# Token tiles turned by VectorE in 32x32 blocks and by transfers inside SBUF, in place of TensorE transposes, in six of eight passes

## What is computed

```python
x = x + 0.5 * ffn0(LN(x))      # silu(x W1^T) * (x W3^T), fast Walsh-Hadamard transform, W2^T; hidden 2048
x = x + attn0(LN(x))           # a second norm with gamma and beta, causal attention, o_proj, its own residual
x = x + 0.5 * ffn0(LN(x))
x = x + 0.5 * ffn1(LN(x))      # ternary weights: silu((x gate^T) gate_s) * ((x up^T) up_s), (down^T) * down_s; hidden 1408
x = x + attn1(LN(x))           # tanh(x B^T) C^T + D * x
x = x + 0.5 * ffn1(LN(x))
```

## Time and profile before

| | us |
|---|---|
| median of 3 runs | 1706.19 |
| lowest, highest | 1705.47, 1707.06 |
| span of the profiled execution | 1703.6 |

### The profile page before, as it was taken

The page is one execution under the profiler, slowest core; times in us unless marked ns, Lnnn a source line. Parts: engine busy times, 40 slices in busy tenths (PEclk is TensorE's granted clock), DMA queues, the critical chain, the costliest instruction groups (busy, mean ns, idle before and its releaser), DMA issues.

```text
span 1703.6 us, 21742 instructions
## 1 busy us (share of the span) xinstructions
PE 1694.7 (99%) x7707; PEld 1401.8 (82%) x7707; DVE 1154.4 (68%) x1808; ACT 830.3 (49%) x1359; POOL 125.5 (7%) x185
## 2 busy tenths in 40 slices
PE   9999999999999999999999999999999999999998
PEld 7788888888888888888888888888888888888887
DVE  8888678677775555754446554447768869877866
ACT  5745444465575543434223333224556556655644
POOL 1000000000012220000000000000000143200001
PEclk9999999999999999999999999999999999999999
DMA  9776665699985000253444433444666763366765
GB/s 317 266 310 247 229 258 211 236 377 369 369 333 207 1 0 1 87 191 126 153 167 167 167 142 136 167 167 146 232 215 211 273 222 112 113 242 234 257 221 213
DMA packets 97341, 344.56 MB, mean 202 GB/s; under 512 B 10192, under 2 KB 25424, under 8 KB 91856
## 3 DMA queue, kind: packets, MB, share of 16 engines
q1 hardware_dynamic: 97232, 343.14, 55.0%
HBM read 261.83 MB, written 81.26 MB: 201 GB/s over the span
## 4 chain that ended last, share of the span: by engine, by line
PE 94%; DVE 3%; DMA 1%; SPq 1%; issue 1%; ACT 0%; DVEq 0%; ACTq 0%
PE psum L561 35%; PE psum L563 30%; PE psum L565 27%; PE psum L857 2%; DMA x<-in_w2a 1%; SPq L705 1%; DVE xc_lo L2074 0%; DMA flat<-in_w3a 0%; DMA w<-w_kept 0%; PE psum L1134 0%; DVE att_lo L2043 0%; DVE fw_lo L2037 0%; SPq L664 0%; DVE x L2020 0%; DVE x L2123 0%
## 5 line engine op out<-in xcount | busy, mean ns | idle before, releaser
L561 PE MATMUL psum<-xc_hi,w 128*128 128x512 f32 x1544 | 604.6, 392 | 0.5 <-DVE psum L2143 0.3
L563 PE MATMUL psum<-xc_lo,w 128*128 128x512 f32 x1544 | 600.9, 389 | 0.0
L565 PE MATMUL psum<-xc_hi,w 128*128 128x512 f32 x928 | 361.3, 389 | 0.0
L561 PEld LDWEIGHTS psum<-xc_hi,w 128*128 128x128 f32 x1544 | 289.8, 188 | 64.4 <-DVE psum L2143 1.6
L563 PEld LDWEIGHTS psum<-xc_lo,w 128*128 128x128 f32 x1544 | 289.9, 188 | 58.8
L561 PE MATMUL psum<-w,hid 128*128 128x512 f32 x864 | 337.5, 391 | 0.0
L565 PE MATMUL psum<-w,hid 128*128 128x512 f32 x864 | 336.4, 389 | 0.0
L2107 DVE TENSOR_TENSOR x<-psum,x 128x512 f32<-128x512 f32 x256 | 173.0, 687 | 148.3 <-PE psum L565 147.7
L563 PE MATMUL psum<-w,hid 128*128 128x512 f32 x544 | 211.7, 389 | 0.0
L565 PEld LDWEIGHTS psum<-xc_hi,w 128*128 128x128 f32 x928 | 174.2, 188 | 36.7
L2131 DVE TENSOR_TENSOR hid<-sg,hid 128x512 fp32r<-128x512 f32 x212 | 144.3, 691 | 85.2 <-ACT hid L1450 83.3
(11 more groups left out here) (177 smaller groups left out, 2030.1 us busy)
## 6 DMA issues: line engine op xcount, KB each, us to landing
w<-w_kept SPq DMA_DIRECT2D x93, 896.0 KB, 6.6
w<-w_kept SPq DMA_DIRECT2D x130, 512.0 KB, 7.1
w<-w_kept SPq DMA_DIRECT2D x57, 640.0 KB, 4.4
w_kept<-w SPq DMA_DIRECT2D x16, 1792.0 KB, 7.3
w<-w_kept SPq DMA_DIRECT2D x93, 256.0 KB, 4.5
w_kept<-prep SPq DMA_DIRECT2D x12, 1792.0 KB, 7.6
w_kept<-w SPq DMA_DIRECT2D x16, 512.0 KB, 6.3
w_kept<-prep SPq DMA_DIRECT2D x12, 512.0 KB, 8.9
```

The source lines that it names most:

```text
L561: pe.matmul(out, a_hi, b_hi, start=start, stop=False, skip_group_check=onto)
L563: last = pe.matmul(out, a_hi, b_lo, start=False, stop=stop and zero == "a", skip_group_check=onto)
L565: last = pe.matmul(out, a_lo, b_hi, start=False, stop=stop, skip_group_check=onto)
```

## The change

Passes 0, 2, 3, 4, 5 and 6 (`SWAPPED`) no longer use TensorE to turn tiles. Pass 1, the attention and the state-space layer keep their transposes.

- VectorE transposes a normalised tile in 32x32 blocks (`swap_pair`, one instruction a tile, two a slot), from xn into the new buffer `swap`, in which the tokens of the pair's two tiles lie alternately (a step of two floats). The pair stands in the slot of its normalisation: in kind B and in A ahead of `sum_c22`, in pass 0 between the two `hid_low`.
- SyncE then moves the blocks to their partitions (`turn_load`): 16 transfers inside SBUF for a pair, each of 32 partitions x 4 runs of 256 B to 32 other partitions, 32 KB. 24 pairs make 384 transfers. In kind B they stand between the first and the later pieces of the weights of slot s+1, at the pair's slot s-1; in kind A and pass 0 behind the slot's loads. They wait for VectorE's swap; the first pair of a kind B pass also for the gates of slot 2, the third and fourth for the down products of slot 4.
- xn has two tiles instead of four; a pair is normalised once the pair before is swapped (in pass 5 also once GpSimd has used it). `norms` of pass 6 become slots 4 to 7.
- The tokens in xs now lie in pairs. Plain order is set where the hidden unit is split: `hid_high` (ScalarE) and `low` (VectorE) read their source with a step of two floats in passes 1, 3, 4, 5, 7 and in the first half of the state-space layer. The planes of xs are renumbered.
- `sums` waits for the transfers. In pass 6 its four steps now stand at the end of slot 8, the start of slot 9, and two at the end of slot 9; in pass 4 they stay.
- ScalarE's 48 copies out of PSUM go.

```diff
-FIRST_SUMS, LAST_SUMS = {8: 0, 9: 2}, {8: 1, 9: 3}
+FIRST_SUMS = {5: {8: (0,), 9: (2,)}, 7: {9: (1,)}}
+LAST_SUMS = {5: {8: (1,), 9: (3,)}, 7: {8: (0,), 9: (2, 3)}}
-NORMS = {4: (3, 4, 5, 6), 5: (4, 5, 6, 7), 6: (4, 4, 5, 6), 7: ()}
+NORMS = {4: (3, 4, 5, 6), 5: (4, 5, 6, 7), 6: (4, 5, 6, 7), 7: ()}
+SWAPPED = (0, 2, 3, 4, 5, 6)
+BLOCK = 32
+LANDED = 16 * 16
-TURNS = {4: (4, 5, 6, 7), 5: (5, 6, 7, 8), 6: (4, 5, 6, 7), 7: ()}
...
+        swap = at("swap", [P, P // BLOCK, KD, BLOCK, 2], F32, "xn", 4 * KIB)
...
+        def in_pairs(tile, no):
+            return tile.rearrange("p (h t i) -> p h i t", h=2, i=2) if paired(no) else tile
...
+                if between:
+                    turn_load(*between)
                 if low_before:
                     w13_low_load(v - 1, block - 1)
                 sp.wait_ge(p4_done, v - 1)
...
+            def turn_load(ps, k):
+                c, cols = k // 2, k % 2 * 2 * P
+                sp.wait_ge(swapped, swaps_before(ps) + 2 * k + 2)
+                if ps.kind == "B" and k == 0:
+                    sp.wait_ge(c22_read, ps.u0 + 3)
+                if ps.kind == "B" and c:
+                    sp.wait_ge(down_ready, ps.downs[4][-1][2] + 1)
+                for a in range(P // BLOCK):
+                    at = slice(cols + a * 2 * BLOCK, cols + (a + 1) * 2 * BLOCK)
+                    for b in range(P // BLOCK):
+                        sp.dma_start(xs[b * BLOCK:(b + 1) * BLOCK, 2 * c:2 * c + 2, :, at].rearrange("p h k t -> p (h k) t"),
+                                     swap[a * BLOCK:(a + 1) * BLOCK, b, :, :, :].rearrange("p k j i -> p k (j i)")).then_inc(turn_in[ps.no], 16)
...
             def turn_tiles(ps, s):
-                    else:
-                        bank_free("n", n)
-                        pe.wait_ge(xn_ready, n + 1)
-                        turn(xn[:, tile % 4, :], plan.bank["n", n]).then_inc(turn_ready, 1)
...
-                for n, tile in ps.turns[s]:
-                    turn_out(n, tile, plan.bank["n", n])
...
+            def swap_pair(ps, k):
+                for j in range(2):
+                    dve.wait_ge(xn_ready, plan.norm_base[ps.no] + 2 * k + j + 1)
+                    if k:
+                        dve.wait_ge(turn_in[ps.no], k * LANDED)
+                    nc.vector.transpose(swap[:, :, :, :, j], xn[:, j, :].rearrange("p (k b t) -> p b k t", k=KD, b=P // BLOCK)
+                                        ).then_inc(swapped, 1)
...
+                if s in ps.norms:
+                    swap_pair(ps, ps.norms.index(s))
                 sum_c22(u)
                 gated(ps, s)
```

More of the change, by code:

```diff
@@ L193, in state_space @@
         self.s_unit, self.s_w2 = self.u, self.w2
-        self.s_downs, self.s_turn = [[] for _ in range(CH)], self.turn
+        self.s_downs, self.s_turn, self.s_norm = [[] for _ in range(CH)], self.turn, self.norm
+        self.norm += PT
         self.uses += -self.uses % 4
@@ L444, in converted, with all_turned, swaps_before, paired @@
             return conv_base(no) + CONVERSIONS[no].index(m) + 1
-        def turns_before(no):
-            return PT * (no + 1 + (no >= BEFORE_S))
+        def all_turned(no):
+            if no == "S":
+                return turn_in[BEFORE_S - 1], PT // 2 * LANDED
+            if no - 1 in SWAPPED and no != BEFORE_S:
+                return turn_in[no - 1], PT // 2 * LANDED
+            return turned, PT * {0: 1, BEFORE_T: 2, BEFORE_S: 3}[no]
+        def swaps_before(ps):
+            return PT * SWAPPED.index(ps.no)
+        def paired(no):
+            return no not in (0, BEFORE_T, BEFORE_S)
+        def of_unit(u):
+            return next(ps.no for ps in passes if ps.u0 <= u < ps.u0 + ps.n)
+        def in_pairs(tile, no):
+            return tile.rearrange("p (h t i) -> p h i t", h=2, i=2) if paired(no) else tile
+        def by_tile(tile, no):
+            return tile.rearrange("p (h i t) -> p h i t", h=2, i=2) if paired(no) else tile
         def hid_of(u, c):
@@ L773, in _ @@
                                  ps.u0 + s - 1 if ps.kind == "B" and s else None, not early,
-                                 ps.kind == "B" and s - 1 in AHEAD)
+                                 ps.kind == "B" and s - 1 in AHEAD,
+                                 (ps, ps.norms.index(s - 1)) if ps.kind == "B" and s - 1 in ps.norms else None)
                     else:
@@ L787, in _ @@
                         w13_low_load(ps.v0 + s + 1, W13_BASE[ps.kind] + s + 1)
+                    if ps.kind == "A" and ps.no in SWAPPED and s in ps.norms:
+                        turn_load(ps, ps.norms.index(s))
                     if ps.no == 1:
@@ L1941, in _ @@
             pool.wait_ge(skip_in, 16)
-            for n, tile in (tt for tiles in passes[BEFORE_S - 1].turns for tt in tiles):
+            for tile in range(PT):
                 if tile == 2:
                     chunk()
-                pool.wait_ge(turn_ready, n + 1)
-                skip(xn[:, tile % TT, :], x[:, tile, :], xn[:, tile % TT, :])
+                pool.wait_ge(swapped, swaps_before(passes[BEFORE_S - 1]) + tile + 1)
+                skip(xn[:, tile % 2, :], x[:, tile, :], xn[:, tile % 2, :])
             chunk()
@@ L2344, in ternary_slot @@
                     return
-                if follower(ps) and s in FIRST_SUMS:
-                    sums(follower(ps), FIRST_SUMS[s])
+                if follower(ps):
+                    for step in FIRST_SUMS[ps.no + 1].get(s, ()):
+                        sums(follower(ps), step)
                 behind = bool(ps.downs[s]) and s not in ps.open
@@ L2359, in ternary_slot @@
                     extra(ps, s, k + 1)
-                if follower(ps) and s in LAST_SUMS:
-                    sums(follower(ps), LAST_SUMS[s])
+                if follower(ps):
+                    for step in LAST_SUMS[ps.no + 1].get(s, ()):
+                        sums(follower(ps), step)
+                if s in ps.norms:
+                    swap_pair(ps, ps.norms.index(s))
                 sum_c22(u)
@@ L2398, in state_low @@
             def state_low(c, j):
-                low(("s", c, j), hid[:, 2 * (c % 2) + j, :, :], sg[:, j, :])
+                low(("s", c, j), hid[:, 2 * (c % 2) + j, :, :], sg[:, j, :], "S" if c < 2 else BEFORE_S)
             def state_x_low(c, i):
```

97 lines of the change are left out of this document (52 added, 45 removed).

## The result

| | before | after |
|---|---|---|
| runs, median (range) | 1706.62 us (1705.47 to 1707.36) | 1757.74 us (1754.81 to 1759.09) |
| profiled span | 1703.6 us | 1756.0 us |
| TensorE's granted clock, mean | 0.999 | 0.986 |
| DMA packets | 97341 | 152638 |

The change makes the kernel slower: the ratio is 1.030, 95% interval 1.0286 to 1.0315. The forecast was 1690.3 us (1684.5 to 1702).

The account below looks back on a forecast made before the run. TensorE was taken to bound the kernel, busy for 1694.7 of 1703.6 us. From 1706.2 us, 21.3 for the removed turns came off and 5.4 for the swap-buffer loop was added: 1690.3 us, range 1684.5 to 1702.

Parts of the forecast that it names:

- the price of a visit: On TensorE, each turn of eight tiles costs 0.89 us; 24 visits removed give back 21.3 us.
- The block turn: On VectorE, two block transposes a swap slot take 1.25 us a pair, between 0.8 and 2.4.
- The stepped splits: The split of hid, read with a two-float step, keeps its 0.69 us on VectorE or doubles.
- The second bound: DMA data in a kind B slot: 8.8 to 10.6 us in all, just full at the upper end.
- The price of an issue: On SyncE's queue, each of the 16 transfers a pair takes 0.47 us to issue, 7.1 to the last issue.
- C: Rival: slower, the loop outgrows the slot by 2.3 us, from 12.3 us on; 1716 or 1724 us; chance 0.12.
- my formula: Kind B: loop of block turns, 15 issues and landing, 10.7 us with wake-ups; loss about 10x - 1.8, so 5.4 us.
- x: In kind B, the loop's time less the slot of 9.98 us; forecast 0.72 us.
- 7.5 us of delay is covered: On SyncE's queue, weights behind the 16 issues are first used more than a slot later, so the delay costs nothing.
- Kind A as free: In kind A and pass 0 the 15 us slot hides the loop of 10.7 us, so no loss there.
- The loop through the swap buffer: VectorE's next swap waits until the previous pair's 16 transfers land; in kind B each further pair is 0.72 us later.
- My 2.4 us for pass 5: In pass 5 slot 4 also finishes tiles, so the whole train is 1.2 us later; loss 2.4 us.

Follow-up runs that it names:

- e12: Changed kernel with 1 transfer of 512 KB a pair in runs of 1 KB, no move between partition groups; 1689.76 us, ratio 0.991.
- e9: Changed kernel with half the issues by GpSimd, a kind A pass's first pair ahead of the second statistics, pass 5 turned on TensorE; 1700.43 us, ratio 0.9953.
- e8: Changed kernel with the 16 transfers a pair reading the input in device memory, not the swap buffer; 1713.71 us, ratio 1.0044.
- e2: Changed kernel with transfers reading a constant tile and VectorE's wait for the landing removed; 1759.99 us, ratio 1.031.
- e5: Changed kernel with swaps only in kind A passes 0, 2 and 3; passes 4 to 6 turn on TensorE as before; 1712.22 us, ratio 1.0029.
- e6: As e5, but in passes 2 and 3 the 16 issues stand behind the next slot's weight loads; 1703.52 us, ratio 0.998.
- e14: As e5, but half of the 16 issues ahead of the next slot's weight loads and half behind; 1732.91 us, ratio 1.016.
- e1: Changed kernel with 4 transfers of 128 KB a pair instead of 16, same bytes and runs, no move between partition groups; 1690.05 us, ratio 0.990.
- e3: Changed kernel with 16 transfers of 32 KB, each 32 packets of 1 KB, no move between partition groups; 1752.21 us, ratio 1.027.
- e4: Changed kernel with 16 transfers of 32 KB, each 128 packets over all 128 partitions, no move between partition groups; 1752.44 us, ratio 1.027.

## Why the prediction was wrong, step by step

**Right.** TensorE's line and the price of a visit: in the changed kernel the first swap slot of passes 2, 3 and 6 is 0.89 to 0.93 us shorter, and with one issue a pair (e12) the span gains 18.1 of the 21.3 us. The block turn: 0.69 us, 1.30 a pair, forecast 1.25. The stepped splits: in the passes that have the step VectorE's median is 692 to 693 ns (691 before) and ScalarE's 657 to 667 (632), so nearly free outside pass 5. The one-element-per-cycle rate for transposes in "Vector Engine (DVE) Microarchitecture Reference" of the Trainium skill, section 3.8, agrees with a block turn that takes no longer than the other instructions of 512 elements. The free step in the Trainium skill's "SBUF — State Buffer", section Door 1, agrees with VectorE's 692 against 691; ScalarE pays some 30 ns. The second bound: I had the data as just full at its upper end, and e9 shows them full (0.99) once the issues are out of the way.

**The price of an issue, 0.47 us.** This is the term that failed first. The rows had 0.43 to 0.70, and I chose by the nearest size and not by the nearest kind: every one of the earlier trace rows reads device memory. With the source in SBUF it is 0.60, and 0.645 from one to the next. The trace of before has no transfer of this kind, so the choice should have stayed open, and C, with this price in its span, should have had more than 0.12. Sixteen take 10.3 to 11.7 us in passes 2 to 6, up to 13.7 in pass 0, and not 7.5.

**But a right price in my formula would not have been enough.** With 1.3 + 15 x 0.645 + 2.0 = 13.0 the loop gives x = 3.0, a loss of 28 and 1713 us; 1757.7 was measured. e8 has nearly my price (in pass 6 8.2 us for 16 on the mean): the formula gives x = 1.4, a loss of 12 and 1697; 1713.7 was measured. Two steps are missing in it.

**"7.5 us of delay is covered", and the queue "just full".** I took the weights as first used more than a slot after their load. In the trace of after TensorE waits for them 28 us in all, and e2, with no loop, loses as much as the whole change, with 44 us of such waits. The sign that I had given for it, gaps with a weight load as the releaser, is there. A queue that needs 14.3 us in a slot of 9.98 isn't a delay to be covered; it adds up from pair to pair. The mechanism stood in the text, as an aside to rival C ("the queue itself is then 14.1 a slot and the weights late as well"); it was priced by the loop alone. (The 14.1 is also a wrong sum: 16 x 0.70 and five loads of 0.47 are 13.6.)

**The clock.** No part of the sum held it. Behind the waits of 2.0 to 5.5 us the granted clock is 0.50 for 3 to 10 us; by the count above 15 of the 52 us.

**Kind A as free.** Wrong for the same reason: the loop has room there (the slot is 15 us), the weights don't. The 10.3 us of issues begin two thirds into the slot, ahead of weights that TensorE needs a slot later and that take up to 7.8 us to land. e5 puts a price on it: 1712 us where 1696 were forecast. Pass 3 alone went from +1.7 to +6.1 in the changed kernel and from -7.4 to -11.0 in e12.

**The loop through the swap buffer.** Real, but not what set the end. Without it nothing is gained (e2). It comes to the front when the weights stand first (e6, e14).

**The skip of pass 5.** I followed SyncE's queue and not GpSimd's. The skip waited for TensorE's turn and now waits for the swap; it moved on to the splits. My 2.4 us for pass 5 were meant for VectorE's crowded slots; e12 loses 4.2 there (from -14.6 to -14.0 in the table, with 3.6 to be given back).

**The rule that spoke against the change.** "DMA: Bandwidth & Descriptors" of the Trainium skill, section Bandwidth, has transfers under 64 KB dominated by their descriptors; my estimate from its 0.95 us was 15 us a pair. The measured 10.3 to 11.7 us lie between that and mine. The price of the issue doesn't go by size here: one of 128 KB takes 0.64 us (e1), one of 512 KB 0.61 (e12), and one of 32 packets about as long as one of 128 (0.59 in e3, 0.60 in e4).

## What to carry to other kernels

Price an issue by a row of the same kind of source, and count a queue's whole slot: the sum of all issues against the length of the slot, and for each load behind the new ones the time until TensorE needs it. What goes over in many small transfers wants fewer of them or a second queue, whose own work in those slots must be followed first. A gap of some 3 us on TensorE was dearer than its length here, since the granted clock fell to 0.50 behind it.

## What the runs showed of the hardware

- An issue from SyncE with an SBUF source takes 0.59 to 0.64 us at the median, whatever it carries (0.59 for 32 partitions x 1 KB, 0.60 for 128 x 256 B and 32 x 4 x 256 B, 0.61 for 512 KB, 0.64 for 512 packets of 256 B); the same transfer with a source in device memory 0.43. From GpSimd it takes 0.55 with an SBUF source.
- 96 or more transfers issued by GpSimd went with 8.6 us from the last addition to the end of the span, none or one with 4.0 to 4.9. Why is open.
- A transfer of 32 KB inside SBUF lands 2.0 us after its issue (median), and 5.8 us where the DMA engines' share is 0.99.
- VectorE's split of 0.69 us, which reads two tiles of SBUF, takes 1.25 to 1.8 us beside GpSimd's work on SBUF; block turns (0.67) and instructions that read PSUM keep their time.
- In the changed kernel's trace TensorE's granted clock was 0.50 for 3 to 10 us behind its waits of 2.0 to 5.5 us.
- With 96 transfers of 16 bytes a partition on their way the DMA engines' share was 1.13 at 179 GB/s, and the kernel lost 28 us.
